# Attention with its maxima in two 64-row halves of the PE array, interleaved causal weighting, and causal masks on VectorE and GpSimd

## What is computed

```
x = x + time_mix(layernorm(x))
x = x + ffn(layernorm(x))        # F: attention without a mask, then experts
x = x + latent(layernorm(x))     # L: causal attention
x = x + ffn(layernorm(x))        # H: as F
# each attention, for 16 heads of 8 features (L: queries and keys folded to this form):
scores = einsum('bqhd,bkhd->bhqk', q, k) / sqrt(8)
attn   = softmax(scores, axis=-1)               # L: only keys k <= q
ctx    = einsum('bhqk,bkhd->bqhd', attn, v)
```

## Time and profile before

| what | value |
|---|---|
| median of 3 runs | 3382.4 us (3379.24 to 3384.87) |
| profiled execution, span | 3382.5 us |
| PE busy | 3032.9 us, 90% |
| DVE busy | 2225.2 us, 66% |
| ACT busy | 1668.8 us, 49% |
| POOL busy | 168.7 us, 5% |
| mean granted TensorE clock | 0.915 |

### The profile page before, as it was taken

How to read it: one execution, slowest core, us unless ns; L and a number is a source line. 1 busy time by engine, 2 the same in 40 slices (tenths; PEclk the granted TensorE clock), 3 DMA queues, 4 the chain that set the end, 5 groups by cost and what they waited for, 6 DMA issues and landing times. The chain is left out here.

```text
span 3382.5 us, 48839 instructions
## 1 busy us (share of the span) xinstructions
PE 3032.9 (90%) x14997; PEld 1205.9 (36%) x14997; DVE 2225.2 (66%) x4191; ACT 1668.8 (49%) x2007; POOL 168.7 (5%) x88
## 2 busy tenths in 40 slices
PE   6788859999999997997799999958999999998998
PEld 2787732222222223443233333322222222222443
DVE  5444459988889893223667666647989888894322
ACT  4212123666666665433255555531666666666333
POOL 1222220000000000001100000011000000000000
PEclk9888866999999997998699999975999999999899
DMA  1000010110011011120111111111010000110211
GB/s 37 1 0 0 0 61 11 29 29 19 27 29 29 17 30 32 69 69 12 59 32 39 30 30 41 30 32 59 15 30 29 29 19 28 29 29 21 76 56 31
DMA packets 75059, 105.46 MB, mean 31 GB/s; under 512 B 17334, under 2 KB 48016, under 8 KB 72433
## 3 DMA queue, kind: packets, MB, share of 16 engines
q1 hardware_dynamic: 71755, 100.97, 9.8%
q10 hardware_dynamic: 3104, 1.94, 0.2%
HBM read 68.72 MB, written 20.55 MB: 26 GB/s over the span
## 5 line engine op out<-in xcount | busy, mean ns | idle before, releaser
L466 DVE TENSOR_REDUCE Hmaxes<-Hm 128x1 f32<-128x512 f32 x1044 | 658.2, 685 | 95.6 <-PE Hm L392 95.0
L466 DVE TENSOR_REDUCE Fmaxes<-Fm 128x1 f32<-128x512 f32 x1044 | 658.1, 685 | 95.5 <-PE Fm L392 95.1
L447 ACT ACTIVATE Hprob<-Hs 128x1024 f32<-128x1024 f32 x512 | 498.5, 1021 | 242.3 <-PE Hs L357 240.7
L447 ACT ACTIVATE Fprob<-Fs 128x1024 f32<-128x1024 f32 x512 | 498.5, 1021 | 242.1 <-PE Fs L357 240.6
L466 DVE TENSOR_REDUCE Lmaxes<-Lm 128x1 f32<-128x512 f32 (+3 forms) x664 | 373.1, 605 | 179.0 <-PE Lm L392 105.3
L447 ACT ACTIVATE Lprob<-Ls 128x1024 f32<-128x1024 f32 (+7 forms) x384 | 293.1, 776 | 268.5 <-PE Ls L360 144.8
L392 PE MATMUL Hm<-Hka,Hqa 99*128 99x512 bf16 x1044 | 381.6, 404 | 27.4 <-DMA Hvh<-Hvstack 11.5
L392 PE MATMUL Fm<-Fka,Fqa 99*128 99x512 bf16 x1044 | 381.4, 404 | 26.8 <-DMA Fvh<-Fvstack 11.0
L357 PE MATMUL Fs<-Fqa,Fka 99*128 99x512 bf16 x1024 | 308.3, 385 | 1.6 <-ACT Fprob L447 1.2
L357 PE MATMUL Hs<-Hqa,Hka 99*128 99x512 bf16 x1024 | 308.2, 384 | 1.6 <-ACT Hprob L447 1.2
L374 PE MATMUL Ho<-Hprob,Hvh 128*32 128x512 f32 x2048 | 276.3, 612 | 0.6 <-ACT Hprob L447 0.6
(11 more groups left out here) (428 smaller groups left out, 2883.7 us busy)
## 6 DMA issues: line engine op xcount, KB each, us to landing
FEwb<-FE_weights SPq DMA_DIRECT2D x8, 1024.0 KB, 5.9
HEwb<-HE_weights SPq DMA_DIRECT2D x8, 1024.0 KB, 5.3
Fqa<-F_qparts SPq DMA_DIRECT2D x51, 96.0 KB
Fka<-F_kparts SPq DMA_DIRECT2D x51, 96.0 KB
Lqa<-L_qparts SPq DMA_DIRECT2D x51, 96.0 KB
Lka<-L_kparts SPq DMA_DIRECT2D x51, 96.0 KB
Hqa<-H_qparts SPq DMA_DIRECT2D x51, 96.0 KB
Hka<-H_kparts SPq DMA_DIRECT2D x51, 96.0 KB
```

What stands on the lines that cost most here:

```text
L447: nc.scalar.activation(prob[:, kt % PSLOTS, q0:q1], sps[SLOT_OF[kt, half]][:, q0 - half * 1024:1024], ACT.Exp, scale=SCALE).then_inc(expd, 1)
L466: nc.vector.reduce_max(maxes[:, qt, kb:kb + 1], src[:, 0:n], AX.X).then_inc(max_free, 1)
```

## The change

The maxima no longer share operands with the scores. They leave out the product of the two smallest parts and use 64 rows: rows 0 to 63 of `qa` and `ka` for even items, rows 64 to 127 of new tensors `qx` and `kx` for odd ones, each with its position in the array (`tile_position=(r, 0)`). The ninth product stands in rows 64 to 71 of `qa`, and the scores still use 99 rows. A step's maxima are issued in even groups ahead of and behind both halves of the scores. The three zero rows are not loaded, as no maximum reads rows 96 to 98. BEFORE is 2.

In L, the query tiles go to the four quarters of the array in turn (tile 4i + g to quarter g). The masks made by matmuls go: on the diagonal, DVE adds a mask and takes the maximum in one call, and GpSimd sets `prob` to zero above the diagonal after the exponential; `weigh` waits for it (`cut`).

```diff
-    LOADS = 16 * (2 * PARTS + 2)
+    LOADS = 16 * (7 + 7 + 1)
     def load_q(sp, h, s):
-        for a in range(PARTS):
-            sp.dma_start(qa[a * PARTS * DH:(a + 1) * PARTS * DH, s, :], qscr[a, bass.ds(h * DH, DH), :].unsqueeze(1)
-                         .broadcast_to([DH, PARTS, T])).then_inc(loaded[s], 16)
-        sp.dma_start(qa[MROW:KROWS, s, :], zero_rows[0:PARTS, :]).then_inc(loaded[s], 16)
+        for r, dst in ((0, qa), (HALF, qx)):
+            for a, copies in ((0, 3), (1, 3), (2, 2)):
+                at = r + 3 * DH * a
+                sp.dma_start(dst[at:at + copies * DH, s, :],
+                             rows(qscr, a, h).unsqueeze(0).broadcast_to([copies, DH, T])).then_inc(loaded[s], 16)
+        sp.dma_start(qa[HALF:HALF + DH, s, :], rows(qscr, 2, h)).then_inc(loaded[s], 16)
...
-    BEFORE = 1
+    BEFORE = 2
...
                         for q0, q1 in blocks(kt, half):
-                            diag = causal and q0 == kt * P
                             o = q0 - half * 1024
-                            last = nc.tensor.matmul(sps[slot][:, o:o + q1 - q0], ka[0:KROWS, s, kt * P:(kt + 1) * P],
-                                                    qa[0:KROWS, s, q0:q1], start=True, stop=not diag)
-                            if diag:
-                                last = nc.tensor.matmul(sps[slot][:, o:o + P], mask_kq[:, :], ident_bf[:, :],
-                                                        start=False, stop=True)
+                            last = nc.tensor.matmul(sps[slot][:, o:o + q1 - q0], ka[0:KROWS, s, keys],
+                                                    qa[0:KROWS, s, q0:q1], start=True, stop=True)
...
                     pe.wait_ge(expd, 2 + h * NHALF + AHEAD[kt + 1])
+                    if causal:
+                        pe.wait_ge(cut, h * NT + kt + 1)
...
+                        if causal:
+                            i0 = -((g - kt) // NB) if kt > g else 0
+                            if i0 == NB:
+                                continue
+                            last = nc.tensor.matmul(
+                                ops[VW * g:VW * (g + 1), i0 * P:BANK], weights,
+                                prob[:, kt % PSLOTS, :].rearrange("p (i g n) -> p i g n", g=NB, n=P)[:, i0:NB, g, :],
+                                start=(kt == 0), stop=(kt == NT - NB + g), tile_position=(0, VW * g))
...
-                    m = nc.tensor.matmul(out[:, 0:n], qa[0:KROWS, s, qt * P:(qt + 1) * P],
-                                         ka[0:KROWS, s, kb * BANK:kb * BANK + n], start=True, stop=not diag)
-                    if diag:
-                        m = nc.tensor.matmul(out[:, n - P:n], mask_qk[:, :], ident_bf[:, :],
-                                             start=False, stop=True)
-                    m.then_inc(max_in, 1)
+                    r = HALF * (j % 2)
+                    qq, kk = ((qx, kx) if r else (qa, ka))
+                    nc.tensor.matmul(out[:, 0:n], qq[r:r + HALF, s, qt * P:(qt + 1) * P],
+                                     kk[r:r + HALF, s, kb * BANK:kb * BANK + n], start=True, stop=True,
+                                     tile_position=(r, 0)).then_inc(max_in, 1)
...
+                        first = (len(items) + 2) // 4 * 2
...
+                        maxima(items[:first])
+                        for half in range(2):
+                            if kt + 1 < NT:
+                                score(h, u, kt + 1, half)
                             elif not last:
-                                score(h + 1, (u + 1) % SLOTS, 0, part)
+                                score(h + 1, (u + 1) % SLOTS, 0, half)
+                        maxima(items[first:])
+                        weigh(h, u, kt)
...
-                    nc.vector.reduce_max(maxes[:, qt, kb:kb + 1], src[:, 0:n], AX.X).then_inc(max_free, 1)
+                    if causal and kb * BANK + n == (qt + 1) * P:
+                        dve.sem_inc(passed, 1)
+                        nc.vector.tensor_tensor_reduce(src[:, 0:n], src[:, 0:n], mask_row[:, BANK - n:BANK], 1.0, 2 * BIG,
+                                                       ALU.add, ALU.max, maxes[:, qt, kb:kb + 1]).then_inc(max_free, 1)
+                    else:
+                        nc.vector.reduce_max(maxes[:, qt, kb:kb + 1], src[:, 0:n], AX.X).then_inc(max_free, 1)
...
+                    with pool.Fori(0, NH) as h:
+                        for kt in range(NT):
+                            pool.wait_ge(expd, 2 + h * NHALF + AHEAD[kt] + 1)
+                            pool.sem_inc(passed, 1)
+                            diag = prob[:, kt % PSLOTS, kt * P:(kt + 1) * P]
+                            nc.gpsimd.affine_select(diag, diag, [[1, P]], ALU.is_ge, none, base=0, channel_multiplier=-1)\
+                                .then_inc(cut, 1)
```

More of the change, by code:

```diff
@@ L277, in attention @@
         y_in = sem("y_in")
+        cut = sem("cut")
+        passed = sem("passed")
         def bank(c):
@@ L366, in weigh @@
                     pe.wait_ge(expd, 2 + h * NHALF + AHEAD[kt + 1])
+                    if causal:
+                        pe.wait_ge(cut, h * NT + kt + 1)
                     if kt == 0:
                         pe.wait_ge(out_sb, h + 1)
+                    weights = vh[:, s, kt * VW:(kt + 1) * VW]
                     for g in range(NB):
-                        q0 = max(first_query(kt), g * BANK)
-                        q1 = (g + 1) * BANK
-                        if q0 >= q1:
-                            continue
-                        last = nc.tensor.matmul(ops[VW * g:VW * (g + 1), q0 - g * BANK:BANK],
-                                                vh[:, s, kt * VW:(kt + 1) * VW], prob[:, kt % PSLOTS, q0:q1],
-                                                start=(kt == 0), stop=(kt == (4 * g + 3 if causal else NT - 1)),
-                                                tile_position=(0, VW * g))
+                        if causal:
+                            i0 = -((g - kt) // NB) if kt > g else 0
[5 more added lines that the diff above has]
+                                start=(kt == 0), stop=(kt == NT - NB + g), tile_position=(0, VW * g))
+                        else:
+                            last = nc.tensor.matmul(ops[VW * g:VW * (g + 1), :], weights,
+                                                    prob[:, kt % PSLOTS, g * BANK:(g + 1) * BANK],
+                                                    start=(kt == 0), stop=(kt == NT - 1), tile_position=(0, VW * g))
                     last.then_inc(weighed, 1)
@@ L412, in head, with maxima @@
                         items = [] if last else share[kt]
-                        for k, part in enumerate((0, 1, "weigh")):
-                            for ahead, j in items[round(len(items) * k / 3):round(len(items) * (k + 1) / 3)]:
+                        first = (len(items) + 2) // 4 * 2
+                        def maxima(part):
+                            for ahead, j in part:
                                 if (ahead, j) == (2, 0):
@@ L513, in _ @@
                 divide(NH - 1)
+            if causal:
+                @block.gpsimd
+                def _(pool):
+                    none = pool.to_reg(0.0)
+                    with pool.Fori(0, NH) as h:
[5 more added lines that the diff above has]
+                                .then_inc(cut, 1)
 E_N, F_N, TOP = 8, 512, 2
```

59 lines of the change are left out of this document (29 added, 30 removed).

## The result

The changed kernel takes 3545.6 us (median of 4 runs, 3533.3 to 3550.3), the kernel before 3382.3: a ratio of 1.0477, 95% interval 1.0457 to 1.0496. It is slower by 163 us where 116 us less was forecast. The profiled execution spans 3548.6 us.

A forecast was written before the change was run, and what follows sets the result against it. TensorE was taken to bound F's and H's loops, with VectorE waiting for it. F -38.5, H -38.5 and L -39 gave -116 us against 3382.5, hence 3266 us, range 3195 to 3335.

The forecast's parts named there:

- F's step: One step of the uncausal attention F on TensorE: 2.59 us against 2.83, with 0.22 per pair and 0.10 per form change.
- rival 1: Maxima pairs: the two array halves do not run together, a pair takes 0.43 us; total 3488 us; 6%.
- rival 2: Form changes to halves cost nothing, so VectorE bounds F's step at 2.48 us; total 3203 us; 14%.
- the loops of F and H: Head loops of the uncausal attentions F and H: -3.0 us per head over fifteen heads, -45 us each.
- rival 3: L's diagonal blocks: GpSimd's cut is slow, 1.4 us with its hand-offs, +54 us; total 3320 us; 9%.
- the 5 us for 28 diagonals: Ahead of L's loop, where VectorE bounds: 28 diagonals cost 0.2 us each in fused add-and-max, +5 us.
- start a head ahead of their use, and the divide's sums behind them have half a head; I cost both at nothing: Loads in the loops: some 10 us of issues instead of 5.4, and the sums queued behind them, cost 0.
- each head would pay up to 4.4: Loops: if the loads' and sums' cover went, the cost would be up to 4.4 us per head.
- the larger loads also delay the store: Start of each attention: reason for the upper end, 8 us, of a forecast +6.5 us (lower end 2.5).
- term (a) of L: Weighing in the causal attention L: interleaving cuts TensorE's work from 14.6 to 10.6 us, -4.0 per head.
- rival 4: Attention loops: the new mix leaves the clock at 1.2 GHz, over +450 us per full attention; 3%.
- the 5.3 that the sum has on TensorE: L, per head: weighing, masks, maxima and form changes together -5.3 us on TensorE, 2.1 of it returning as waits.

The follow-up runs named there:

- kernel 8: Kernel 6 with a plain reduce instead of the fused add-and-max on L's diagonal blocks; 3296.4 us.
- kernel 3: The changed kernel with 12 instead of 24 of a causal head's 40 maxima two heads ahead, so its loads are used later; 3526.2 us.
- kernel 5: The changed kernel with VectorE's divide at three quarters of a head's maxima instead of half; 3467.6 us.
- kernel 1: The changed kernel with its loads' rows ordered features outermost, as before the change, instead of copies outermost; 3333.9 us.
- kernel 9: Kernel 6 with the causal attention's turn behind four maxima of the next head instead of two; 3281.7 us.
- kernel 14: Kernel 1 with L's weighing not interleaved; 3354.8 us.
- kernel 10: Kernel 9 with L's weighing not interleaved, each group weighing 512 queries in a row; 3267.8 us.
- kernel 6: Kernel 1 with the divide at three quarters of a head and 12 instead of 24 causal maxima two heads ahead; 3283.7 us.
- kernel 15: Kernel 10 with TensorE's and VectorE's loops written out head by head; 3211.7 us.
- kernel 13: Kernel 10 with the causal head's maxima spread more evenly over its steps (planner's constant 1600 instead of 400); 3278.7 us.

## Why the prediction was wrong

**Right.** F's step came out at 2.61 for 2.59, with the pairs side by side and 0.10 per change of form; rivals 1 and 2 are out. Once the loads are mended, the loops of F and H gain 39.5 and 40.2 of the 45 forecast, VectorE's idle time ahead of F's reduces is 53.2 (under 45 was expected), and the starts grow by 6.6, 6.1 and 4.5 for 6.5. The cut and the fused maxima are cheap, and rival 3 is out; the 5 us for 28 diagonals ahead of L's loop were too much (1 us, kernel 8).

**The step that failed** is "start a head ahead of their use, and the divide's sums behind them have half a head; I cost both at nothing". I counted issues (10 us for 5.4) and rows, not what the loads need to land. The diff turns the loads round, copies ahead of features, and I read that as a matter of rows only. Worse, "a head ahead of their use" is false in L: the order has the first maximum of the head after next in step 4 of 16, and TensorE comes to it 11 to 15 us behind the first issue. Held against that, my own 10 us of issues left next to nothing for the landing. The divide's "half a head" was no cover either (kernels 3 and 5). The fallback, "each head would pay up to 4.4", was again the issues' difference; L's heads take 8.2 us longer (43.8 for 35.6 from turn to turn, where 32.4 was forecast), as half-clock stretches follow the waits. The same omission made the starts +18 where 8 was the upper end: "the larger loads also delay the store" named the right mechanism, and sized it too small. The change against kernel 1 has 38 us of this in the starts (12.0, 12.1 and 13.6), 105 in L's loop and 72 in those of F and H, together 214 of the 217 us between the two profiled executions.

The Trainium skill had this: "DMA: Bandwidth & Descriptors", in Rules for kernel authors, says that a DMA uses no more engines than its outermost dimension has entries, where these are fewer than 16, and names a leading broadcast of copies as the case. The trace agrees: 4.6 engines are busy with mostly 3 and 2 entries outermost, 9.9 with 8. These are means over several loads in flight behind a store; no row shows one load alone. I weighed the page on tiling, which spoke of the form changes, and not this one.

**Second, smaller:** term (a) of L, -4.0 per head by weighing. At full clock 2.3 of it came; a whole head of L takes 30.4 us at full clock in kernel 9 and 35.0 in the kernel before, 4.6 less, near the 5.3 that the sum has on TensorE. But of the weighing's term only 0.9 per head is left in the change's schedule (kernels 1 and 14) and nothing in the mended one (9 and 10). My rival 4 asked whether the clock would rise; it rose, and then fell again and again. With loads, use and divide mended, kernel 6 has L's loop at 518.8, -25.6 for -48, and the whole at 3283.7, inside the range, 18 above the forecast. That it is so near is in part luck: kernel 6 also has a schedule that the prediction did not cost, and 6 us less ahead of L's loop by it. The step on TensorE was priced rightly; the transfers that feed it were not in the sum, nor was the clock's fall in L.

## What to carry to other kernels

When an edit rewrites a load, compare the access pattern's outermost dimension, and not its bytes alone; then find the first instruction that needs it in the order, and what stands behind it on its queue. Where two waits lie behind the same slow transfers, removing one shows the other, as in kernel 3. And a saving on TensorE counts only at the clock that is granted: a head of kernel 10 is 2.3 us longer than one of kernel 9 when both are at full clock, and yet its loop is no longer.

## What the hardware showed unexpectedly

In the change a wait of 1.36 us of VectorE at the divide was followed by 6.8 us at 0.50. The gaps at the loop's end, 2.6 us each in kernel 10, cost F about 5.5 us each (22 us for four by kernel 15), more than twice themselves. In kernel 9 the clock also fell in L's late steps, where no wait of TensorE was longer than 0.59 us in the rows shown, while kernel 13, without the interleaving and with as much waiting for VectorE, was granted 0.99. Writing the loop out for TensorE and VectorE, 15 heads in a row, brought no wait of TensorE in F's loop that is put down to issue, where kernel 10 has four.
